# Top-four router of a decoder layer: choice by match and replace instead of indices, and another order of VectorE's work

## What is computed

```
logits = x @ router_w + router_b                 # 16 per row
probs = softmax(logits)
topw, topi = top_k(probs, 4);  topw /= sum(topw)
combine = sum(one_hot(topi, 16) * topw[..., None])
out = sum over e of combine[:, e] * (gelu(x @ w1[e] + b1[e]) @ w2[e] + b2[e])
x = layernorm(x + out)
```

## Time and profile before

| | us |
|---|---|
| median of 3 runs | 618.67 |
| profiled execution, span from first to last instruction | 611.2 |
| TensorE matmul busy | 535.9 |
| VectorE busy | 419.1 |
| ScalarE busy | 336.2 |
| GpSimd busy | 289.8 |
| the 64 row transfers of `dispatch` on GpSimd | 63.3 |

### The profile page before, as it was taken

How to read it: one execution, slowest core, us unless ns; L and a number is a source line. 1 busy time by engine, 2 the same in 40 slices (tenths; PEclk the granted TensorE clock), 3 DMA queues, 4 the chain that set the end, 5 groups by cost and what they waited for, 6 DMA issues and landing times.

```text
span 611.2 us, 14540 instructions
## 1 busy us (share of the span) xinstructions
PE 535.9 (88%) x4048; PEld 501.5 (82%) x4048; DVE 419.1 (69%) x973; ACT 336.2 (55%) x650; POOL 289.8 (47%) x264
## 2 busy tenths in 40 slices
PE   5999999999779999999648999999999999999600
PEld 4978888888668888887537999999999999999600
DVE  2646655555467888866546888888788888888236
ACT  2433333333235555545236787878778787778404
POOL 5551111111120656656630457676767777676633
PEclk9999999999989999978657999999999999999955
DMA  8799999900000223222379799999999999998477
GB/s 282 258 386 384 385 385 386 367 0 0 1 1 2 107 84 112 77 100 89 121 220 330 214 258 262 266 253 259 263 265 256 262 251 257 268 259 208 47 195 241
DMA packets 91834, 127.70 MB, mean 209 GB/s; under 512 B 6736, under 2 KB 62992, under 8 KB 91808
## 3 DMA queue, kind: packets, MB, share of 16 engines
q1 hardware_dynamic: 76320, 107.22, 53.5%
q0 software_dynamic: 14592, 19.93, 16.0%
q10 hardware_dynamic: 896, 0.23, 0.2%
HBM read 62.58 MB, written 64.78 MB: 208 GB/s over the span
## 4 chain that ended last, share of the span: by engine, by line
PE 75%; issue 7%; DVE 5%; DMA 4%; POOL 4%; ACT 3%; SPq 1%; ACTq 0%; POOLq 0%; DVEq 0%
PE ps L345 19%; PE ps L347 18%; PE ps L346 18%; PE ps L949 3%; POOL expert_rows L558 3%; PE ps L821 2%; PE ps L829 2%; PE ps L768 2%; PE ps L839 1%; PE ps L890 1%; PE ps L817 1%; DMA xg<-expert_rows 1%; PE ps L800 1%; PE ps L882 1%; DMA x_all<-in_x 1%
## 5 line engine op out<-in xcount | busy, mean ns | idle before, releaser
L602 POOL DMA_INDIRECT expert_sum<-yb,home_row x80 | 167.4, 2093 | 103.5 <-DVE home_row L1514 81.7
L345 PE MATMUL ps<-gT_h,w_h 128*128 128x256 f32 x320 | 94.8, 296 | 1.6 <-issue 1.3
L345 PE MATMUL ps<-w_h,h_h 128*128 128x256 f32 x320 | 90.7, 283 | 1.2 <-DVE h_l L1507 1.2
L347 PE MATMUL ps<-gT_h,w_l 128*128 128x256 f32 x320 | 91.6, 286 | 0.0
L346 PE MATMUL ps<-gT_l,w_h 128*128 128x256 f32 x320 | 91.4, 286 | 0.0
L346 PE MATMUL ps<-w_l,h_h 128*128 128x256 f32 x320 | 90.6, 283 | 0.0
L347 PE MATMUL ps<-w_h,h_l 128*128 128x256 f32 x320 | 90.5, 283 | 0.0
L1507 DVE TENSOR_TENSOR h_l<-hf,h_h 128x1024 fp32r<-128x1024 f32 x40 | 49.0, 1226 | 37.9 <-ACT h_h L1155 37.9
L558 POOL DMA_INDIRECT expert_rows<-x_all,idx x64 | 63.3, 989 | 19.0 <-issue 17.2
L1148 ACT ACTIVATE hf<-ps,b1s 128x256 f32<-128x256 f32 x160 | 62.9, 478 | 9.3 <-PE ps L347 8.9
L345 PEld LDWEIGHTS ps<-gT_h,w_h 128*128 128x128 f32 x320 | 62.5, 195 | 2.2 <-issue 1.5
(11 more groups left out here) (238 smaller groups left out, 1330.7 us busy)
## 6 DMA issues: line engine op xcount, KB each, us to landing
expert_rows<-zeros SPq DMA_DIRECT2D x32, 1152.0 KB, 14.3
w1f<-in_L_ffn_w SPq DMA_DIRECT2D x40, 512.0 KB, 4.7
w2f<-in_L_ffn_w SPq DMA_DIRECT2D x40, 512.0 KB, 5.9
xg<-expert_rows SPq DMA_DIRECT2D x40, 288.0 KB, 3.8
total<-expert_sum SPq DMA_DIRECT2D x16, 256.0 KB, 6.1
x_all<-in_x SPq DMA_DIRECT2D x8, 256.0 KB, 7.0
expert_sum<-x_all SPq DMA_DIRECT2D x8, 256.0 KB
expert_sum<-total SPq DMA_DIRECT2D x4, 512.0 KB
```

What stands on the lines that cost most here:

```text
L345: pe.matmul(o, ah, bh, start=first, stop=False)
L347: return pe.matmul(o, al, bh, start=False, stop=last)
L602: pool.indirect_dma_start(out=sums[p], out_offset=bass.IndirectOffsetOnAxis(ap=home_row[:, p, c:c + 1], axis=0), in_=yb[:, p, c], in_offse ...
```

## The change

The four chosen experts of a row are found in another way. The logits tile gets four more columns with a very low value, and the tile of the eight largest four such values ahead of them. `match_replace` replaces in the logits the values that equal one of eight (the four low ones and the four largest logits) by another low value; where the result differs from the logits, the mask is one. The places of a row are then the four largest of mask times (place + 1), found by `max` over 16, less one; carry and the thresholds of the table are one higher for that. The index tile, its cast, the one-hot of 4 x 16 and both reductions over 64 elements are gone.

The shares are written once, into x_all. ScalarE copies them from there into a packed tile (`pack_shares`), the first half in the round of tile 12, between the exponentials of the logits and those of the attention, the second half at the end; TensorE's transposes of the shares wait for these copies.

VectorE's list has another order: share_sum stands ahead of var2, and var2 ahead of all_shares. From round 17 on VectorE goes by a third list, `ending`.

```diff
-            for skew, fn in ramp if t < ramp_steps else stages:
+            for skew, fn in ramp if t < ramp_steps else ending if ending and t > n else stages:
...
-            sp.wait_ge(z_ok, 2)
+            sp.wait_ge(z_ok, 1)
...
-            pool.memset(shares[:], 0.0).then_inc(z_ok, 1)
             pool.wait_ge(c_pool, 24)
...
+            pool.memset(lg[:, :, E:E + PAD], LOWEST).then_inc(low_ok, 1)
+            pool.memset(mx8[:, :, 0:PAD], LOWEST).then_inc(low_ok, 1)
...
             def turn_shares(half, bank):
+                pe.wait_ge(sh_in, half + 1)
...
-                    pe.wait_ge(lst, done(NT // 2 - 1))
                     turn_shares(0, 0)
...
+            def pack_shares(half):
+                act.wait_ge(lsh, done(half * (NT // 2) + NT // 2 - 1))
+                act.activation(shares[:, half].rearrange("p b (a e) -> p b a e", e=2 * E),
+                               x_all[:].rearrange("p (b a) c -> p b a c", b=B)[:, :, half * 4:half * 4 + 4, D:RW], ACT.Copy).then_inc(sh_in, 1)
...
+                if isinstance(t, int) and t == NT - 4:
+                    pack_shares(0)
                 if isinstance(t, int) and t == NT - 2:
                     turned_shares(0, 0)
...
-            def chosen(t, p, k):
+            def without_top(t, p, k):
+
                 dve.wait_ge(l8, done(t))
                 dve.sem_inc(passed, 1)
-                dve.max_index(ix8[:, p], mx8[:, p], lg[:, p]).then_inc(li8, 1)
...
-                dve.tensor_tensor(oh[:, p], iota16[:].unsqueeze(1).broadcast_to([P, K, E]),
-                                  ixf[:, p].unsqueeze(2).broadcast_to([P, K, E]), ALU.is_equal).then_inc(loh, 1)
+                dve.match_replace(rest[:, p], mx8[:, p, 0:8], lg[:, p], TAKEN).then_inc(lrest, 1)
 
             def chosen_mask(t, p, k):
...
-                    dve.tensor_reduce(mk[:, p], oh[:, p].rearrange("p r e -> p e r"), AX.X, ALU.add).then_inc(lmk, 1)
+                dve.tensor_tensor(mk[:, p], rest[:, p, 0:E], lg[:, p, 0:E], ALU.not_equal).then_inc(lmk, 1)
...
-                dve.scalar_tensor_tensor(shares[:, ds(p * TPB + k, 1), 0:E].rearrange("p a e -> p (a e)"), lexp[:, p], winv[:, p:p + 1],
-                                         f(mk[:, p]), ALU.mult, ALU.mult).then_inc(lst, 1)
...
-                dve.tensor_tensor(ohp[:, p], oh[:, p], pos[:, p].unsqueeze(1).broadcast_to([P, K, E]), ALU.mult).then_inc(lohp, 1)
+                dve.tensor_tensor(posm[:, p], pos[:, p], f(mk[:, p]), ALU.mult).then_inc(lpm, 1)
...
-                dve.tensor_reduce(slotf[:, p], ohp[:, p], AX.X, ALU.add).then_inc(lsl, 1)
+                dve.max(at8[:, p], posm[:, p]).then_inc(lat, 1)
...
-                dve.tensor_copy(idx[:, ds(t, 1), :].rearrange("p a r -> p (a r)"), slotf[:, p]).then_inc(lidx, 1)
+                dve.tensor_scalar(idx[:, ds(t, 1), :].rearrange("p a r -> p (a r)"), at8[:, p, 0:K], -1.0, None, ALU.add).then_inc(lidx, 1)
...
-            pipeline(dve, NT, [(3, head_inv), (5, rows_of), (3, head_norm), (5, next_rows), (5, pick_rows), (5, slots), (5, indices),
-                               (1, head_max), (4, logits_out), (4, largest), (1, sub_max), (3, residual2), (4, chosen), (3, stats2),
-                               (4, chosen_float), (3, aggr2), (4, one_hot), (3, var2), (4, chosen_mask), (4, share_sum), (4, all_shares),
-                               (3, norm2)])
+            pipeline(dve, NT, [(3, head_inv), (5, rows_of), (3, head_norm), (5, next_rows), (5, chosen_rows), (5, slots), (5, indices),
+                               (1, head_max), (4, logits_out), (4, largest), (1, sub_max), (3, residual2), (4, without_top), (3, stats2),
+                               (4, chosen_mask), (3, aggr2), (4, share_sum), (3, var2), (4, all_shares), (3, norm2)],
+                     ending=[(5, rows_of), (5, next_rows), (5, chosen_rows), (5, slots), (5, indices), (3, head_inv), (3, head_norm),
+                             (4, logits_out), (4, largest), (4, without_top), (4, chosen_mask), (4, share_sum), (4, all_shares),
+                             (3, residual2), (3, stats2), (3, aggr2), (3, var2), (3, norm2)])
```

More of the change, by code:

```diff
@@ L66, in score_bank, with pipeline @@
     return 4 if isinstance(t, int) and t == 0 else 2 * p
-def pipeline(eng, n, stages, ramp=None, ramp_steps=0):
+def pipeline(eng, n, stages, ramp=None, ramp_steps=0, ending=None):
     depth = max(skew for skew, _ in stages)
@@ L153, in decoder_layer @@
         idx = sb("idx", [P, NT, K], U32)
-        shares = sb("shares", [P, NT, 2 * E])
+        shares = sb("shares", [P, 2, B, 4 * 2 * E])
         b2s = sb("b2s", [P, D])
@@ L219, in decoder_layer @@
         x2T = sbe("x2T", [P, 2, KD, P])
-        lg = sbe("lg", [P, 2, E])
+        lg = sbe("lg", [P, 2, E + 8 - K])
+        rest = sbe("rest", [P, 2, E + 8 - K])
         lmax = sbe("lmax", [P, 2])
@@ L491, in _ @@
             pool.wait_ge(c_pool, 20)
-            pool.tensor_scalar(carry[:], iota16[:], float(CAP), 0.0, ALU.mult, ALU.add).then_inc(c_pool, 1)
+            pool.tensor_scalar(carry[:], iota16[:], float(CAP), 1.0, ALU.mult, ALU.add).then_inc(c_pool, 1)
             pool.memset(zeros[:], 0.0).then_inc(c_pool, 1)
@@ L851, in turn_shares @@
             def turn_shares(half, bank):
+                pe.wait_ge(sh_in, half + 1)
                 for b in range(B):
-                    a = b * TPB + half * 4
-                    mm = pe.transpose(ps[:, bank, b * P:(b + 1) * P], shares[:, a:a + 4], ident[:])
+                    mm = pe.transpose(ps[:, bank, b * P:(b + 1) * P], shares[:, half, b], ident[:])
                 mm.then_inc(sh_pe, 1)
@@ L1098, in rexps @@
                 act.wait_ge(lsh, freed(t))
-                act.activation(lexp[:, p], lg[:, p], ACT.Exp, bias=lmax[:, p:p + 1]).then_inc(lex, 1)
+                act.activation(lexp[:, p], lg[:, p, 0:E], ACT.Exp, bias=lmax[:, p:p + 1]).then_inc(lex, 1)
+                if isinstance(t, int) and t == NT - 4:
+                    pack_shares(0)
                 if isinstance(t, int) and t == NT - 2:
@@ L1104, in top_sum @@
                 act.wait_ge(lwi, freed(t))
-                act.activation(top[:, p], mx8[:, p, 0:K], ACT.Exp, bias=lmax[:, p:p + 1], accum_out=wsum[:, p:p + 1]).then_inc(lws, 1)
+                act.activation(top[:, p], mx8[:, p, PAD:PAD + K], ACT.Exp, bias=lmax[:, p:p + 1], accum_out=wsum[:, p:p + 1]).then_inc(lws, 1)
             pipeline(act, NT, [(4, x2_turned), (4, keep_x2), (3, o_out), (2, p_out), (4, neg_max), (4, rexps), (1, cexps), (4, top_sum), (0, q_out)],
@@ L1111, in _ @@
             act.dma_start(b1r[:], b1).then_inc(ld_c, 16)
+            pack_shares(1)
             turned_shares(1, 6)
@@ L1362, in logits_out @@
                 dve.wait_ge(lex, freed(t))
-                dve.tensor_tensor(lg[:, p], ps[:, 5, LG:LG + E], rb[:], ALU.add).then_inc(lgb, 1)
+                dve.tensor_tensor(lg[:, p, 0:E], ps[:, 5, LG:LG + E], rb[:], ALU.add).then_inc(lgb, 1)
             def largest(t, p, k):
@@ L1369, in largest @@
                 dve.sem_inc(passed, 1)
-                dve.max(mx8[:, p], lg[:, p]).then_inc(l8, 1)
-            def chosen(t, p, k):
+                dve.max(mx8[:, p, PAD:PAD + 8], lg[:, p, 0:E]).then_inc(l8, 1)
+            def without_top(t, p, k):
                 dve.wait_ge(l8, done(t))
                 dve.sem_inc(passed, 1)
-                dve.max_index(ix8[:, p], mx8[:, p], lg[:, p]).then_inc(li8, 1)
-            def chosen_float(t, p, k):
-                dve.wait_ge(li8, done(t))
-                dve.tensor_copy(ixf[:, p], ix8[:, p, 0:K]).then_inc(lif, 1)
-            def one_hot(t, p, k):
-                dve.wait_ge(lif, done(t))
-                dve.tensor_tensor(oh[:, p], iota16[:].unsqueeze(1).broadcast_to([P, K, E]),
-                                  ixf[:, p].unsqueeze(2).broadcast_to([P, K, E]), ALU.is_equal).then_inc(loh, 1)
+                dve.match_replace(rest[:, p], mx8[:, p, 0:8], lg[:, p], TAKEN).then_inc(lrest, 1)
             def chosen_mask(t, p, k):
-                dve.wait_ge(loh, done(t))
+                dve.wait_ge(lrest, done(t))
                 dve.wait_ge(pos_ps, freed(t))
-                with nc.allow_low_precision(reason="a sum of zeros and at most a one is exact"):
-                    dve.tensor_reduce(mk[:, p], oh[:, p].rearrange("p r e -> p e r"), AX.X, ALU.add).then_inc(lmk, 1)
+                dve.tensor_tensor(mk[:, p], rest[:, p, 0:E], lg[:, p, 0:E], ALU.not_equal).then_inc(lmk, 1)
             def share_sum(t, p, k):
```

34 lines of the change are left out of this document (17 added, 17 removed).

## The result

| | median us | runs | of them in us |
|---|---|---|---|
| before | 620.22 | 4 | 618.01 to 622.00 |
| changed | 627.56 | 4 | 625.16 to 630.12 |

The ratio is 1.019, with a 95% interval of 1.0145 to 1.0235. It is not the quotient of these medians, 1.012, since it takes in runs in the fast state alone; it points to a base of about 615.9 us, near the medians of 616.75 to 617.36 that the kernel before has beside most of the experiments. The sign is right and 627.56 lies in the forecast's range, but only because the base of 618.67 was high: 1.019 times 618.67 is 630.4, above the range. The loss is larger than forecast, by ratio 1.9% instead of 1.1%. Taken again beside three experiments it was 630.98 against 617.26, ratio 1.0186 (1.0138 to 1.0235).

A forecast was written before the change was run, and what follows sets the result against it. The prediction took TensorE to bound the kernel (75% of the span); 4.0 us up to round 16 plus 2.7 in the tail, 6.7 added to 618.67, gave 625.4 us, own range 624.4 to 627.8, wider range 621.8 to 629.5.

The forecast's parts named there:

- the base of 618.67: Whole kernel: median time in us of the runs before the change, to which the forecast added 6.7 us.
- one profiled span and a constant: Whole kernel: the profiled span of 611.2 us, with the median of the runs taken to stand 7.5 above it.

## What to carry to other kernels

An instruction that is cheap and whose inputs are ready still costs what the wait ahead of it in its queue costs; ask of each reordered instruction which other engine's result now stands in front of it, and follow the waiter through its own chain, here VectorE, GpSimd, VectorE, TensorE. When such a chain leaves a nearly full TensorE idle for a few tenths of a microsecond per round, price the clock as well: the runs' granted clock gives the exchange rate, here 0.45 to 0.5 us for each at 1.2 GHz. And set a forecast on the difference of paths and of clock time, not on one profiled span and a constant.

## What the runs showed that I had not expected

TensorE gave back 10.8 us for two more matmuls per round whose result nobody reads (630.98 to 620.19). With 0.45 us of idle time in a round of 7.5, so 94% busy, the clock fell two or three times in rounds 4 to 16; with that time filled, it did not fall there. The spread of the kernel before, 608 to 622 us, goes for the most part with its time at 1.2 GHz, 70 to 98 us; 3.7 us of spread are left when half of that time is taken off.
